# Local attention: the values products one step later on TensorE, the copy of the transposed probabilities after the exponentials on ScalarE

## The chip, the cores and the metric

One core of a Trainium2 chip (trn2). The metric is the device time of one launch in microseconds; the time before is the median of 3 runs. Engines are named as in the profile: PE (TensorE matmul), PEld (its weight loads), DVE (VectorE), ACT (ScalarE), POOL (GpSimd), SP (SyncE, which issues the DMAs here).

## The reference, cut to what matters

`x` is 16 batches of 256 tokens with 128 features. A first phase does one cross-attention over 1601 keys. The second phase, in which everything of this change lies, runs six layers of local attention and a gated FFN:

```python
for i in range(DEPTH):                                   # 6
    x = attn_layer(shift_tokens(x), Wqkv[i], ...) + x
    x = ffn_layer(shift_tokens(x), ...) + x

def attn_layer(x, Wqkv, qs, ksc, Wo):                    # 16 heads of 64
    q, k, v = jnp.split(x @ Wqkv, 3, -1)
    q, k = l2norm(q) * qs, l2norm(k) * ksc               # then rotated by position
    out = local_attention(q, k, v)                       # windows of 32, own and previous
    return out @ Wo

def local_attention(q, k, v):
    sim = jnp.einsum('bhwie,bhwje->bhwij', bq, bk2) * QK_SCALE
    attn = jax.nn.softmax(jnp.where(mask, -big, sim), -1)
    return jnp.einsum('bhwij,bhwje->bhwie', attn, bv2)
```

## The kernel before, in words

The program is written engine by engine. Each engine runs its own list of instructions in order, and semaphores tie the lists together. In the second phase all engines step through the same function `iteration(A, B, C, D)`: four batches are in flight, one in each role. A is projected to q, k and v, squared for its norms and rotated. B has its scores and softmax. C gets the tail of its attention, the output product and the start of its FFN. D gets the end of its FFN. Roles shift by one batch for each iteration: 6 layers of 16 batches make 96 iterations with a B.

An iteration has 8 steps `k`. The attention of a batch is cut into 8 units of four heads by 128 queries; units 0 to 3 (t = 0) are the first half of the tokens, 4 to 7 (t = 1) the second. Unit `u` goes through five stages, and `unit_at(B, C, k, lag)` says which unit stands in step `k` at a stage that lags by `lag` steps (below zero it is one of C):

- `scores` (PE, L1360 and L1369, tiles of 64*64 of the array) writes bank `b_sc`, in step u. The 8 products have 128 columns for t = 0 and 96 for t = 1, as has the mask product ahead of them in each pair (256 and 192).
- DVE takes the maxima (L1268) and makes the biases `nb` (L1277); then ACT does four exponentials with their sums (L1144), in step u. They wait for `nb_ready`, and for `pt_done` of unit u-2, since `probs` has two buffers.
- DVE inverts the sums (L1213) and POOL scales the probabilities (L1068), lag 1.
- `transposes` (PE, L1381, 128*128) turns them into bank `b_pt`, of which there is one; ACT copies it to `probsT` (L1131), which has two buffers. Lag 2.
- `values` (PE, L1401, tiles of 128*64) multiplies `probsT` with `v` into half of the bank `b_o` (the half by u % 2): 8 products of 64 columns for t = 1, 4 of 128 for t = 0; the trace shows each fp32 product as two matmuls. Lag 2. DVE copies `b_o` to `oT` after each second unit (L1205, `keep_o`, lag 3, even steps), and an even unit waits for the copy before it (`o_kept`).

Around these stand, on PE: the projections of A (L1442 in steps 0 to 3, L1453 in 4 to 7), the norms (L1417, steps 2 and 4), the transposed norms (L1464, step 5), the last FFN product of D (L1473, step 0), the output product of C (L1483, steps 1 and 3), two LayerNorm products (L1488, L1492, steps 4 and 5) and the first FFN product (L1513, steps 6 and 7). On ACT: the squares (L1158), logarithm and exponential of the norms (L1109, L1116), copies of v (L1166), and once per iteration the Gelu (L1183) between two loads of a function table (L1183, L79), of which the second stands ahead of the exponentials of step 0. On DVE: the rotations (L1247, L1253), the copy `oT` and the vector parts of the FFN, as `xg` (L1302).

Of the kernel before, what the change touches and what calls it, by code (L numbers as in the profile page):

```python
# [14 lines left out]
ACT = mybir.ActivationFunctionType  # L15
# [753 lines left out]
def ffn_phase(nc, xn_scr, x1_scr, rk_scr, ident, identb, ins, out, NB, DEPTH):  # L769
    with ExitStack() as ctx:  # L770
# [37 lines left out]
        probsT = sb("probsT", [P, 2, 512])  # L808
# [51 lines left out]
        def count(name, n, c, back=0):  # L860

            return n * per[name] + (AHEAD - back) * per[name] + c
# [6 lines left out]
        def unit_at(B, C, k, lag):  # L869

            return (B, k - lag) if k >= lag else (C, UNITS + k - lag)
# [222 lines left out]
        @block.scalar  # L1094
        def _(act):
            s = sems
            start_ahead(act, "act")
            act.wait_ge(setup, N_SETUP)
            act.wait_ge(consts_in, 16 * N_CONSTS)
            nc.scalar.activation(gate_t[:, :], gate[:, :], ACT.Tanh).then_inc(gate_ready, 1)  # L1100
            load_tables(nc, act, EXP_LN_TABLES)

            def iteration(A, B, C, D, begin=None):
                def inverse_norms(i, dst):
                    n = A[0]
                    act.wait_ge(s["norm_done"], count("norm_done", n, i + 1))

                    act.wait_ge(s["rn_ready"], count("rn_ready", n, i))
                    nc.scalar.activation(ln_n2[:, :], b_nv[:, :], ACT.Ln, bias=eps_c[:, 1:2],  # L1109
                                         scale=LN_SCALE).then_inc(s["ln_ready"], 1)  # L1110
                    act.wait_ge(s["ln_ready"], count("ln_ready", n, i + 1))
                    if i == 0:
                        act.wait_ge(s["rk_out"], count("rk_out", n, 0))
                    else:
                        act.wait_ge(s["rqt_done"], count("rqt_done", n, 0))
                    nc.scalar.activation(dst[:, :], ln_n2[:, :], ACT.Exp, bias=eps_c[:, 2:3],  # L1116
                                         scale=-0.5).then_inc(s["rn_ready"], 1)

                for k in range(STEPS):
                    if C and k == 5:  # L1120
                        n = C[0]
                        act.wait_ge(s["xc_done"], count("xc_done", n, 1))
                        act.wait_ge(s["var_done"], count("var_done", n, 1, back=1))
                        nc.scalar.activation(xsq[:, :], b_c[:, S:2 * S], ACT.Square).then_inc(s["xsq_ready"], 1)
                    row, u = unit_at(B, C, k, 2)
                    if row:
                        n = row[0]
                        act.wait_ge(s["pt_done"], count("pt_done", n, u + 1))

                        act.wait_ge(s["o_done"], count("o_done", n, u - 1))  # L1130
                        nc.scalar.activation(probsT[:, u % 2, :], b_pt[:, :], ACT.Copy).then_inc(s["pt_kept"], 1)  # L1131
                    if D and k == 0:

                        load_tables(nc, act, EXP_LN_TABLES)
                    if B:
                        n, _, p, _ = B
                        t, j0 = k // 4, 2 * (k % 4)
                        c0, w = C0[t], P - C0[t]
                        act.wait_ge(s["nb_ready"], count("nb_ready", n, k + 1))

                        act.wait_ge(s["pt_done"], count("pt_done", n, k - 1))
                        for e in range(2):
                            for h in range(2):
                                last = nc.scalar.activation(  # L1144
                                    probs[:, t, k % 2, 2 * e + h, c0:P], b_sc[:, 512 * e + h * w:512 * e + (h + 1) * w],
                                    ACT.Exp, bias=nb[:, k % 2, e, h:h + 1], scale=rq[:, p, t, j0 + h, e:e + 1],
                                    accum_out=psums[:, k % 2, 2 * e + h:2 * e + h + 1])
                        last.then_inc(s["exp_ready"], 1)
                    if A and k == 2:
                        inverse_norms(0, rn_k)  # L1150
                    if A and k < 4:
                        n = A[0]
                        for i in (2 * k, 2 * k + 1):

                            act.wait_ge(s["rotc_ready"], count("rotc_ready", n, i + 1))

                            act.wait_ge(s["norm_done"], count("norm_done", n, i // 4))
                            nc.scalar.activation(sq[:, i % 4, :], b_qk[:, 512 * (i % 2):512 * (i % 2 + 1)], ACT.Square  # L1158
                                                 ).then_inc(s["sq_ready"], 1)
                    if A and 4 <= k < 7:  # L1160
                        n, _, p, _ = A
                        i, e = k - 4, k % 2

                        act.wait_ge(s["o_done"], count("o_done", n, UNITS, back=2))
                        act.wait_ge(s["v_done"], count("v_done", n, i + 1))
                        nc.scalar.activation(v[:, p, i // 2, e * 512:(e + 1) * 512], b_qk[:, e * 512:(e + 1) * 512],  # L1166
                                             ACT.Copy).then_inc(s["v_kept"], 1)
                    if A and k == 4:
                        inverse_norms(1, rn_q)
                    if C and k == 5:  # L1170
                        n = C[0]
                        act.wait_ge(s["var_done"], count("var_done", n, 1))
                        act.wait_ge(s["rstd_ready"], count("rstd_ready", n, 1, back=1))
                        nc.scalar.activation(ln_v[:, :], b_c[:, 0:S], ACT.Ln, bias=eps_c[:, 0:1]
                                             ).then_inc(s["lnv_ready"], 1)
                        act.wait_ge(s["lnv_ready"], count("lnv_ready", n, 1))
                        act.wait_ge(s["xg_ready"], count("xg_ready", n, 1, back=1))
                        nc.scalar.activation(rstd[:, :], ln_v[:, :], ACT.Exp, scale=-0.5).then_inc(s["rstd_ready"], 1)
                if C:
                    n = C[0]  # L1180
                    act.wait_ge(s["h_kept"], count("h_kept", n, 3))
                    act.wait_ge(s["hh_ready"], count("hh_ready", n, 1, back=1))
                    nc.scalar.activation(gg[:, :], gt[:, :], ACT.Gelu).then_inc(s["gelu_ready"], 1)  # L1183
            rows(act, lambda layer: None, iteration)
# [156 lines left out]
        def _(pe):  # L1341
            s = sems
# [4 lines left out]
            def iteration(A, B, C, D, begin=None):  # L1347
# [36 lines left out]
                def values(row, u):  # L1384
                    n, _, p, _ = row
                    t, j0 = u // 4, 2 * (u % 4)
                    pe.wait_ge(s["v_kept"], count("v_kept", n, 3))
                    pe.wait_ge(s["v3_kept"], count("v3_kept", n, 1))
                    if t == 1:
                        pe.wait_ge(s["vmid_in"], count("vmid_in", n, 32))  # L1390

                    pe.wait_ge(s["o_kept"], count("o_kept", n, u // 2))
                    pe.wait_ge(s["pt_kept"], count("pt_kept", n, u + 1))
                    for h in range(2):
                        o0 = (u % 2) * 2 * P + h * P
                        for tile, q0, q1 in V_USE[t]:
                            for e in range(2):
                                r = slice(e * DH, (e + 1) * DH)
                                vc = slice((2 * (j0 + h) + e) * DH, (2 * (j0 + h) + e + 1) * DH)
                                c = (2 * e + h) * P  # L1400
                                last = nc.tensor.matmul(b_o[r, o0 + q0:o0 + q1], v[:, p, tile, vc],  # L1401
                                                        probsT[:, u % 2, c + q0:c + q1], start=True, stop=True,
                                                        skip_group_check=True)
                    last.then_inc(s["o_done"], 1)
# [16 lines left out]
                for k in range(STEPS):  # L1421
                    if B:
                        scores(k)
                    row, u = unit_at(B, C, k, 2)
                    if row:
                        transposes(row, u)
# [33 lines left out]
                    if A and k == 5:  # L1460
# [2 lines left out]
                        for i in range(4):  # L1463
                            last = nc.tensor.transpose(b_nv[:, i * P:(i + 1) * P], rn_q[:, i * P:(i + 1) * P], ident[:, :])  # L1464
                        last.then_inc(s["rqt_done"], 1)
                    if row:
                        values(row, u)
                    if D and k == 0:
                        n, loaded = D[0], D[3]
                        pe.wait_ge(part_in[PART_2], loaded)  # L1470
# [199 lines left out]
```

## Time and profile before

| | us |
|---|---|
| median of 3 runs | 5797.53 (5788.45 to 5801.63) |
| the profiled execution | 5784.99 |
| its span | 5783.2 |
| stretch of the second phase, 2100 to 5700 of the span | 3600.00 |
| PE busy in it | 3478.76 |
| ACT busy in it | 2883.59 |
| DVE busy in it | 2226.03 |
| POOL busy in it | 2194.72 |

The first phase ends at about 2040. From there on PE is the fullest engine. Its granted clock was 1.00 in the stretch. "Busy" counts matmuls from start to a modelled end, so neighbouring groups overlap a little: the time that a group takes is read from its start to the start of the next. A row of the timeline gives the start, the time from the first start to the last end, engine and line, the shapes, and in brackets how long the engine sat idle before and what ended that.

### The profile page before, as it was taken

Reading aid. Unit: us, or ns where it says so; the run is one execution under the profiler, and the core shown is the slowest. Engines: PE = TensorE matmul, PEld = TensorE weight load, DVE = VectorE, ACT = ScalarE, POOL = GpSimd, SP = SyncE. Lnnn points to the kernel's source line nnn. Section 1 sums busy time; section 2 is a strip of 40 time slices with the busy share of each in tenths; the row PEclk is TensorE's granted clock in tenths of the full one; section 3 lists DMA queues with packets and bytes.
Section 4 is the critical chain, followed back from the end, with each engine's and each line's share of the span. In section 5 each row is a group of like instructions: output and inputs, shape, how many; then the busy total and the mean of one; then the engine's idle time right before and its main releaser. Section 6 shows DMA issues by size and latency. Waiting matters only on the chain.

```text
span 5783.2 us, 146589 instructions
## 1 busy us (share of the span) xinstructions
PE 5490.1 (95%) x51848; PEld 3278.6 (57%) x51848; DVE 3631.9 (63%) x8009; ACT 3995.5 (69%) x10790; POOL 2653.2 (46%) x2284
## 2 busy tenths in 40 slices
PE   5999999999999789999999999999999999999997
PEld 2444444444444356666666666666666666666665
DVE  3666776677667456666666666666666666656664
ACT  2555555555555478787887778787888788878885
POOL 2211221112211166656665666666666666665663
PEclk9999999999999899999999999999999999999999
DMA  3232222222332133333333333333333333333332
GB/s 85 61 71 74 57 73 67 74 64 66 74 75 63 54 103 97 100 104 108 97 100 99 108 100 101 94 109 103 102 93 108 104 104 93 97 115 103 93 98 89
DMA packets 144825, 517.35 MB, mean 89 GB/s; under 512 B 29884, under 2 KB 46140, under 8 KB 125676
## 3 DMA queue, kind: packets, MB, share of 16 engines
q1 hardware_dynamic: 142572, 507.58, 31.0%
q8 instruction: 427, 7.00, 0.5%
q14 instruction: 290, 2.38, 0.1%
q10 hardware_dynamic: 1536, 0.40, 0.0%
HBM read 224.98 MB, written 30.68 MB: 44 GB/s over the span
## 4 chain that ended last, share of the span: by engine, by line
PE 44%; ACT 12%; issue 6%; DVE 2%; POOL 1%; DMA 0%; SPq 0%; ACTq 0%; DVEq 0%; POOLq 0%
PE b_qk L1442 9%; PE b_c L1483 6%; PE b_pt L1381 5%; PE b_o L1401 5%; ACT probs L1144 5%; PE b_sc L1369 4%; PE b_nv L1417 3%; PE b_qk L1453 3%; PE b_sc L1360 2%; ACT L1183 2%; ACT L79 2%; PE b_c L1513 2%; PE b_nv L1513 1%; ACT ln_n L1109 1%; PE b_c L1488 1%
## 5 line engine op out<-in xcount | busy, mean ns | idle before, releaser
L436 ACT ACTIVATE eT<-b_e 128x512 f32<-128x512 f32 (+1 forms) x1664 | 903.2, 594 | 871.5 <-PE b_e L754 751.2
L1144 ACT ACTIVATE probs<-b_sc,nb,rq 128x96 f32<-128x96 f32 (+1 forms) x3072 | 1322.5, 449 | 8.7 <-DVE nb L1277 7.5
L509 DVE CUSTOM_DVE_ANT_0 junk<-b_s,mq 128x1024 bf16<-128x1024 f32 (+1 forms) x1024 | 998.9, 990 | 373.3 <-PE b_s L736 359.1
L1068 POOL TENSOR_TENSOR probs<-probs,rsums 128x512 f32<-128x512 f32 (+1 forms) x768 | 717.2, 934 | 666.4 <-DVE rsums L1213 665.9
L1268 DVE TENSOR_REDUCE b_sc<-b_sc 128x4 f32<-128x512 f32 (+1 forms) x768 | 486.1, 633 | 837.6 <-PE b_sc L1369 837.5
L1131 ACT ACTIVATE probsT<-b_pt 128x512 f32<-128x512 f32 x768 | 455.9, 594 | 579.7 <-PE b_pt L1381 579.7
L1442 PE MATMUL b_qk<-xs,weights 128*128 128x256 f32 x3072 | 740.3, 384 | 59.5 <-ACT sq L1158 31.8
L750 PE MATMUL b_e<-mk,identb 128*128 128x512 bf16 (+1 forms) x1664 | 636.7, 383 | 20.6 <-ACT eT L436 19.9
L1144 ACT ACTIVATION_READ_ACCUMULATOR probs<-b_sc,nb,rq 128x1 f32 x3072 | 645.9, 210 | 0.0
L754 PE MATMUL b_e<-q_op,k_op 75*128 75x256 bf16 (+1 forms) x3328 | 639.8, 273 | 0.0
L1442 PEld LDWEIGHTS b_qk<-xs,weights 128*128 128x128 f32 x3072 | 556.4, 191 | 144.9 <-issue 74.5
L1401 PEld LDWEIGHTS b_o<-probsT,v 128*64 128x64 f32 x9216 | 373.0, 137 | 453.3 <-issue 453.3
L1247 DVE TENSOR_TENSOR rot_s<-b_qk,rot_tab 128x512 f32<-128x512 f32 x768 | 525.3, 684 | 127.2 <-PE b_qk L1442 114.7
L1037 POOL TENSOR_TENSOR kT<-kT,rot_p 128x1024 f32<-128x1024 f32 x192 | 454.6, 2368 | 306.1 <-DMA rot_p<-rot_s 302.5
L1401 PE MATMUL b_o<-probsT,v 128*64 128x64 f32 (+1 forms) x9216 | 515.7, 247 | 34.2 <-DVE oT L1205 26.9
L736 PE MATMUL b_s<-k_op,q_op 72*128 72x512 bf16 (+1 forms) x2048 | 504.0, 343 | 27.2 <-DVE smax L509 13.7
L1158 ACT ACTIVATE sq<-b_qk 128x512 f32<-128x512 f32 x768 | 439.1, 599 | 125.1 <-DVE kT L1253 65.5
L656 PE MATMUL b_pv<-eT,vx 128*9 128x256 f32 x6656 | 518.1, 383 | 2.8 <-ACT eT L436 2.8
L1381 PE MATMUL b_pt<-ident,probs 128*128 128x128 f32 x3072 | 504.0, 287 | 1.1 <-POOL probs L1068 1.1
L1045 POOL TENSOR_TENSOR kT<-kT,rkb 128x1024 f32<-128x1024 f32 x192 | 452.1, 2355 | 110.8 <-DMA rkb<-rk_scr 110.8
L1037 POOL TENSOR_TENSOR qT<-qT,rot_p 128x1024 f32<-128x1024 f32 x192 | 453.0, 2359 | 89.5 <-DMA rot_p<-rot_s 70.4
L754 PEld LDWEIGHTS b_e<-q_op,k_op 75*128 75x128 bf16 (+1 forms) x3328 | 332.4, 100 | 252.5 <-issue 5.2
(133 smaller groups left out, 8348.8 us busy)
## 6 DMA issues: line engine op xcount, KB each, us to landing
rot_p<-rot_s SPq DMA_DIRECT2D x768, 256.0 KB, 2.4
rkb<-rk_scr SPq DMA_DIRECT2D x192, 512.0 KB, 6.4
k_op<-k_scr SPq DMA_DIRECT2D x192, 300.2 KB
v<-v SPq DMA_DIRECT2D x192, 256.0 KB, 3.6
k_scr<-kp SPq DMA_DIRECT2D x48, 400.2 KB, 3.5
weights<-in_ffn_w SPq DMA_DIRECT2D x27, 512.0 KB, 5.0
ctxT<-in_ctx SPq DMA_DIRECT2D x17, 800.5 KB, 8.7
q_op<-q_scr SPq DMA_DIRECT2D x144, 64.0 KB
```

Source lines behind the costliest of these rows:

```text
L436: nc.scalar.activation(eT[0:n, g % 2, i * 512:(i + 1) * 512], b_e[i][0:n, :], ACT.Exp).then_inc(s["e_ready"], 1)
L509: nc.vector.tensor_tensor_reduce(junk[:, half, 0:n], b_s[u % 2][:, 0:n], mq[:, p, qt, half * 1024:half * 1024 + n], 1.0, LOWEST, ALU.add, ...
L656: last = nc.tensor.matmul(b_pv[32 * h:32 * h + DK + 1, 0:S], vx[0:n, p, kt, 4 * q + h, :], eT[0:n, g % 2, h * S:(h + 1) * S], start=(kt == ...
L750: nc.tensor.matmul(b_e[i][0:n, :], identb[0:n, 0:n], mk[0:n, p, kt, :].unsqueeze(1).to_broadcast([n, 2, S]), start=True, stop=False, skip_ ...
L754: last = nc.tensor.matmul(b_e[i][0:n, j * S:(j + 1) * S], k_op[q][0:MROW + 3, 2 * i + j, kt * P:kt * P + n], q_op[0:MROW + 3, p, 4 * q + 2 ...
L1037: nc.gpsimd.tensor_tensor(dst, dst, rot_p[:, i % 2, :].rearrange("p (j t) -> p j t", j=4), ALU.add).then_inc(s["sum_ready"], 1)
L1068: nc.gpsimd.tensor_tensor(pu, pu, rsums[:, u % 2, :].unsqueeze(2).to_broadcast([P, 4, w]), ALU.mult).then_inc(s["pn_ready"], 1)
L1144: last = nc.scalar.activation(probs[:, t, k % 2, 2 * e + h, c0:P], b_sc[:, 512 * e + h * w:512 * e + (h + 1) * w], ACT.Exp, bias=nb[:, k % ...
L1247: nc.vector.tensor_tensor(per_block(rot_s[:, q % 2, 512 * (i % 2):512 * (i % 2 + 1)]), per_block(src), rot_tab[:, tab + 1, :].unsqueeze(1) ...
L1381: last = nc.tensor.transpose(b_pt[:, i * P:(i + 1) * P], probs[:, t, u % 2, i, :], ident[:, :])
L1401: last = nc.tensor.matmul(b_o[r, o0 + q0:o0 + q1], v[:, p, tile, vc], probsT[:, u % 2, c + q0:c + q1], start=True, stop=True, skip_group_c ...
L1442: last = nc.tensor.matmul(b_qk[:, 512 * (i % 2) + x * S:512 * (i % 2) + (x + 1) * S], weights[:, c0:c0 + P], xs[:, p, :], start=True, stop ...
```

## The change

Two pieces of code move, and nothing is added or taken away. On PE `values` now has lag 3, and stands right behind `scores` of the step instead of behind the projections. On ACT the copy to `probsT` stands behind the exponentials of its step instead of before them.

```diff
@@ scalar engine, step k
-                    row, u = unit_at(B, C, k, 2)
-                    if row:
-                        n = row[0]
-                        act.wait_ge(s["pt_done"], count("pt_done", n, u + 1))
-
-                        act.wait_ge(s["o_done"], count("o_done", n, u - 1))
-                        nc.scalar.activation(probsT[:, u % 2, :], b_pt[:, :], ACT.Copy).then_inc(s["pt_kept"], 1)
                     if D and k == 0:
 
                         load_tables(nc, act, EXP_LN_TABLES)
...
                         last.then_inc(s["exp_ready"], 1)
+                    row, u = unit_at(B, C, k, 2)
+                    if row:
+                        n = row[0]
+                        act.wait_ge(s["pt_done"], count("pt_done", n, u + 1))
+
+                        act.wait_ge(s["o_done"], count("o_done", n, u - 1))
+                        nc.scalar.activation(probsT[:, u % 2, :], b_pt[:, :], ACT.Copy).then_inc(s["pt_kept"], 1)
                     if A and k == 2:
                         inverse_norms(0, rn_k)
@@ tensor engine, step k
                     if B:
                         scores(k)
+                    row, u = unit_at(B, C, k, 3)
+                    if row:
+                        values(row, u)
                     row, u = unit_at(B, C, k, 2)
                     if row:
                         transposes(row, u)
...
-                    if row:
-                        values(row, u)
                     if D and k == 0:
```

On PE, steps 7 and 0 of one iteration and the next stood before as follows (`b_sc` scores, `b_pt` transposes, `b_qk` projections of A, `b_o` values, then FFN products of C and D):

```order
8711 L1360 MATMUL b_sc<-lmask,identb 64x192 x4
8712 L1369 MATMUL b_sc<-kT,qT 64x96 x8
8713 L1381 MATMUL b_pt<-ident,probs 128x128 x4
8714 L1453 MATMUL b_qk<-weights,xs 128x512
8715 L1401 MATMUL b_o<-probsT,v 64x64 x8
8716 L1513 MATMUL b_c<-xg,weights 128x256 x2
8717 L1360 MATMUL b_sc<-lmask,identb 64x256 x4
8718 L1369 MATMUL b_sc<-kT,qT 64x128 x8
8719 L1381 MATMUL b_pt<-ident,probs 128x128 x4
8720 L1442 MATMUL b_qk<-xs,weights 128x256 x4
8721 L1401 MATMUL b_o<-probsT,v 64x64 x8
8722 L1473 MATMUL b_nv<-hT,weights 128x256 x3
```

The same two steps in the changed kernel, whose lines are shifted by up to three:

```order
8761 L1360 MATMUL b_sc<-lmask,identb 64x192 x4
8762 L1369 MATMUL b_sc<-kT,qT 64x96 x8
8763 L1401 MATMUL b_o<-probsT,v 64x64 x8
8764 L1381 MATMUL b_pt<-ident,probs 128x128 x4
8765 L1456 MATMUL b_qk<-weights,xs 128x512
8766 L1514 MATMUL b_c<-xg,weights 128x256 x2
8767 L1360 MATMUL b_sc<-lmask,identb 64x256 x4
8768 L1369 MATMUL b_sc<-kT,qT 64x128 x8
8769 L1401 MATMUL b_o<-probsT,v 64x64 x8
8770 L1381 MATMUL b_pt<-ident,probs 128x128 x4
8771 L1445 MATMUL b_qk<-xs,weights 128x256 x4
8772 L1474 MATMUL b_nv<-hT,weights 128x256 x3
```

In every step the values products stand ahead of the transposes now, and are those of the unit before; the projections are followed directly by the 128*128 products that the values stood in front of.

On ACT the same place, from the exponentials of step 7 (96 columns) to those of step 0 (128 columns), stood before as follows (`probsT` the copy, `gg` the Gelu):

```order
1541 L1131 ACTIVATE probsT<-b_pt 128x512
1542 L1144 ACTIVATE probs,psums<-b_sc,nb,rq 128x96 x4
1543 L1183 ACT_TABLE_LOAD
1544 L1183 ACTIVATE gg<-gt 128x768
1545 L1131 ACTIVATE probsT<-b_pt 128x512
1546 L79 ACT_TABLE_LOAD
1547 L1144 ACTIVATE probs,psums<-b_sc,nb,rq 128x128 x4
1548 L1158 ACTIVATE sq<-b_qk 128x512 x2
```

In the changed kernel:

```order
1541 L1137 ACTIVATE probs,psums<-b_sc,nb,rq 128x96 x4
1542 L1148 ACTIVATE probsT<-b_pt 128x512
1543 L1183 ACT_TABLE_LOAD
1544 L1183 ACTIVATE gg<-gt 128x768
1545 L79 ACT_TABLE_LOAD
1546 L1137 ACTIVATE probs,psums<-b_sc,nb,rq 128x128 x4
1547 L1148 ACTIVATE probsT<-b_pt 128x512
1548 L1158 ACTIVATE sq<-b_qk 128x512 x2
```

Between the first exponentials of step 7 and the first of step 0 there is still one copy; it moved from behind the Gelu to ahead of the first table load, and the copy ahead of step 7's exponentials has gone behind them.

## Rows read from the trace of the kernel before

**Rows 1.** The head of the page: span and instructions.
```profile
span 5783.2 us, 146589 instructions
```

**Rows 2.** Waits of PE, 2100 to 5700: us in total, times, longest.
```profile
PE b_sc L1360 <- ACT probs L1144: 57.8, 89, 0.7
PE b_qk L1442 <- ACT sq L1158: 27.3, 93, 0.3
PE b_o L1401 <- DVE oT L1205: 22.9, 93, 0.3
```

**Rows 3.** Timeline of PE, step 7 of an iteration to step 1 of the next.
```profile
4004.13 0.28 PE L1360 MATMUL b_sc<-lmask,identb 64*64 64x192 bf16 x4
...
4004.67 0.66 PE L1381 MATMUL b_pt<-ident,probs 128*128 128x128 f32 x4
4005.16 1.02 PE L1453 MATMUL b_qk<-weights,xs 128*128 128x512 f32 x2
4006.11 0.69 PE L1401 MATMUL b_o<-probsT,v 128*64 128x64 f32 x16
4006.73 1.13 PE L1513 MATMUL b_c<-xg,weights 128*128 128x256 f32 x4
4007.87 0.30 PE L1360 MATMUL b_sc<-lmask,identb 64*64 64x256 bf16 x4
...
4011.50 1.53 PE L1473 MATMUL b_nv<-hT,weights 128*128 128x256 f32 x6
4013.69 0.30 PE L1360 MATMUL b_sc<-lmask,identb 64*64 64x256 bf16 x4 [0.65 <-ACT probs L1144]
```

**Rows 4.** Timeline of ACT, the same steps 7 and 0.
```profile
4005.36 0.60 ACT L1131 ACTIVATE probsT<-b_pt 128x512 f32<-128x512 f32 x1 [2.10 <-PE b_pt L1381]
4005.85 0.43 ACT L1144 ACTIVATE probs<-b_sc,nb,rq 128x96 f32<-128x96 f32 x1
...
4008.93 0.84 ACT L1183 ACTIVATE gg<-gt 128x768 f32<-128x768 f32 x1
4009.68 0.58 ACT L1131 ACTIVATE probsT<-b_pt 128x512 f32<-128x512 f32 x1
...
4011.57 0.46 ACT L1144 ACTIVATE probs<-b_sc,nb,rq 128x128 f32<-128x128 f32 x1
```

**Rows 5.** Timeline of PE, the steps 2 to 7 that follow.
```profile
4022.20 1.07 PE L1417 MATMUL b_nv<-sq,pair_ones 128*32 128x512 f32 x8
...
4025.40 1.97 PE L1442 MATMUL b_qk<-xs,weights 128*128 128x256 f32 x8 [0.29 <-ACT sq L1158]
...
4034.02 0.28 PE L1360 MATMUL b_sc<-lmask,identb 64*64 64x192 bf16 x4
...
4035.05 1.02 PE L1453 MATMUL b_qk<-weights,xs 128*128 128x512 f32 x2
4035.91 0.60 PE L1464 MATMUL b_nv<-ident,rn_q 128*128 128x128 f32 x4
...
4037.77 0.28 PE L1360 MATMUL b_sc<-lmask,identb 64*64 64x192 bf16 x4
...
4040.07 0.69 PE L1401 MATMUL b_o<-probsT,v 128*64 128x64 f32 x16 [0.25 <-DVE oT L1205]
4040.69 1.13 PE L1513 MATMUL b_c<-xg,weights 128*128 128x256 f32 x4
4041.66 1.03 PE L1513 MATMUL b_nv<-xg,weights 128*128 128x256 f32 x4
```

**Rows 6.** Timeline of ACT, norms and first square of steps 2 and 3.
```profile
4023.33 0.69 ACT L1109 ACTIVATE ln_n<-b_nv,eps_c 128x512 f32<-128x512 f32 x1 [0.40 <-PE b_nv L1417]
...
4024.68 1.06 ACT L1158 ACTIVATE sq<-b_qk 128x512 f32<-128x512 f32 x2
```

**Rows 7.** Timeline of DVE, step 6.
```profile
4039.12 0.69 DVE L1205 COPY oT<-b_o 128x512 f32<-128x512 f32 x1
4039.73 0.47 DVE L1302 SCALAR_TENSOR_TENSOR xg<-b_c,par,rstd 128x256 f32<-128x256 f32 x1
```

## The prediction

> **What bounds the kernel now.** I read the page first: the span is 5783.2 [rows 1], and the change touches only the part behind 2040. There PE leads with 3478.76 busy of 3600, so I asked for the waits of PE in that stretch. Three rows hold nearly all of them [rows 2]: scores that wait for exponentials (57.8 us), projections that wait for squares (27.3) and values that wait for the copy `oT` (22.9). Each comes some 93 times, once in an iteration, so the timeline of one iteration stands for all.
>
> Step 7 takes 3.74 from scores to scores (4004.13 to 4007.87), step 0 takes 5.82 [rows 3]. The reader is to see that PE works without a gap through step 0 until 4013.03 (4011.50 + 1.53) and then sits idle for 0.65 until ACT is through with the exponentials of step 0. ACT is late there because of a chain without slack from step 7 on: exponentials from 4005.85, load, Gelu at 4008.93, copy at 4009.68, load, exponentials at 4011.57 [rows 4]. The scores of step 0 too start as soon as ACT lets them: exponentials start 4005.85, scores 4007.87, which is 2.02 for four exponentials and the signal. Step 5 (4034.02 to 4037.77, 3.75) is the third of that kind. So of 8 steps, three (7, 0, 5) have the length of the loop scores, DVE and transposes, ACT, scores; the others have the length of PE's own work plus, in steps 3 and 6, one wait.
>
> **The change part by part.** No instruction is added, so the sum consists of starts that shift.
>
> *Steps 7 and 0.* Before, the exponentials started behind the copy: transposes at scores + 0.54, their end 0.66 later, copy, exponentials at scores + 1.72 [rows 3, 4]. Now the copy is out of the way, but the transposes stand behind the values, and the exponentials wait for these transposes (`pt_done`). A values group takes 0.62 from start to next start (4006.11 to 4006.73) [rows 3]. So: 0.54 + 0.62 + 0.66 + 0.03 for the signal (transposes end 4005.33, copy starts 4005.36) = 1.85 after the scores. What was 1.72 becomes 1.85: **+0.13**. The copy that stood in front took 0.49 (4005.36 to 4005.85), the values take 0.62; it is these two that are exchanged. From there to the exponentials of step 0 ACT has the same work as before, one copy, two loads and the Gelu, only in another order: 5.72 (4005.85 to 4011.57) stays [rows 4]. So the 0.65 on PE before step 1 is not won: the copy no longer stands behind the Gelu, but it stands ahead of the first load. The two steps together get 0.13 longer.
>
> The Gelu gets later by a copy, some 0.5 + 0.13, with respect to the scores of step 7. DVE's part of the FFN hangs on it and on its own `oT` copy, and the product L1473 on that. It may move from 4011.50 by some 0.2 to 0.3, but PE has 0.65 of idle time behind it, so this costs nothing; with that cover gone it would cost just these 0.2 to 0.3 in each iteration.
>
> *Step 5.* The same exchange: 0.54 + 0.62 + 0.66 + 0.03 + 2.02 = 3.87 instead of 3.75: **+0.12** [rows 3 to 5].
>
> *Step 6.* Values of an even unit wait here for `oT`, 0.25 by the row, and start at scores + 2.30 (4037.77 to 4040.07) [rows 5]. The new unit in step 6 is odd and stands in the half of `b_o` that was freed long ago: this wait goes. What is late next is `xg`, for which L1513 waits: DVE ends it at 4040.20 (4039.73 + 0.47) [rows 7]. From DVE's end to PE's start the row of `oT` shows 0.26 (4039.12 + 0.69 = 4039.81 to 4040.07) [rows 5, 7]. So L1513 could start at 4040.46 at the latest, by PE's own work at 4040.28 (37.77 + 0.54 + 0.62 + 0.49 transposes + 0.86 projection), against 4040.69 before: between -0.23 and -0.41. I take **-0.30**, a little off the late end. `oT` itself now waits for values of its own step; these end at scores + 1.2 and DVE comes to `oT` at + 1.35 (4037.77 to 4039.12), so it isn't delayed, by 0.1.
>
> *Steps 1 and 3.* These have PE's own length. Their sequence was scores (64*64), transposes and projections (128*128), values (128*64), output product (128*128); now it is scores, values, transposes, projections, output product: one change of tile shape fewer. What such a change costs is in the rows. The projection L1453 to the next group takes 0.95 where values follow (4005.16 to 4006.11), and 0.86 where 128*128 follows (4035.05 to 4035.91) [rows 3, 5]: 0.09 for leaving. And the first four matmuls of L1513 behind values take 1.13, the next four 1.03 [rows 5]: 0.10 for entering. Together **-0.20** in each of these steps, -0.40 for both. The same is won in step 6 (it is in its number) and in 7, 0 and 5, where the loop through ACT hides it. In steps 2 and 4 the norms (128*32) stand between, and the number of changes stays. Bounds: nothing (if the change into 128*64 behind 64*64 costs more than others) and twice as much.
>
> The Trainium skill says this too: on the page "TensorEngine Tiling (Array Packing)", section "Key Properties", a change of tiling mode drains the engine, a change of tile within a mode doesn't. Without a cost for it the sum below would be smaller by 0.40 an iteration; the rows above agree with the page, with 0.09 and 0.10.
>
> The wait of step 3 stays. The projections at 4025.40 wait for squares, these for the norms: norms start 4022.20, logarithm 4023.33, squares 4024.68, projection 4025.40 [rows 5, 6]. Norms are later by 0.62 in their step, and the projection would be too, as values now stand before each; the 3.20 between them are ACT's. ACT was idle 0.40 before the logarithm [rows 6], and the copy falls into that.
>
> *Step 2* gets a unit of the second half with 16 small matmuls instead of 8 larger ones, +0.03; *step 4* nothing. In all steps below 4 the projections, and with them the rotations on DVE, the swap DMAs and POOL's sums, come 0.62 later. Nothing waits closely for them: the squares of step 1 end well before the norms of step 2, POOL's products are due some 3 us later.
>
> **The sum.** +0.13 + 0.12 - 0.30 - 0.40 + 0.03 = -0.42 us an iteration. Over 93 full iterations [rows 2] -39 us. The profiled execution (5784.99, 1.8 above its span [rows 1]) would come to 5746; it is 12.5 below the median of the runs, and from the median 5797.5 I get **5758**.
>
> **The rivals.**
>
> 1. *Shape changes are free in effect* (what is left of -0.42 without the -0.40 is nothing): 5796. For it: the gain rests on 0.1 us effects seen in other neighbourhoods. Against: each is seen in every iteration.
> 2. *Values behind scores cost no drain, and the exponentials follow sooner.* If values can start while the last scores run, 0.1 less in all steps, those of the ACT loop too: -0.8 more an iteration, 5797.5 - 93 * 1.2 = 5685. Against: the transposes behind the same scores start 0.54 after them, at their modelled end less 0.07.
> 3. *Slower: the waits of the values become visible.* `values` has up to five semaphores to pass (both kinds of v, its swapped part, `o_kept`, `pt_kept`). Before, PE's sequencer passed them while the long projections ran; now they stand behind the scores, the shortest group (0.54). A wait that PE meets with an empty queue costs 0.26 (the `oT` row). Half of it exposed in 7 steps is +0.91, net +0.49 an iteration, 5843; all of it +130 us, 5927. It decides from 0.06 a step (0.42 / 7). Against it: the transposes, with two, start behind the same scores without delay. The Trainium skill bears on it in one sentence, "Perfetto Trace Analysis", section "Identifying Dependency Chains": waits beyond one may become instructions of their own ahead of the waiting one; the page gives no price, so by it alone the sum stays.
> 4. *Slower: the later projections find somebody.* The 0.62 later rotations, swaps or sums reach a wait that has no slack. Each 0.45 an iteration cancels the gain: about 5800 to 5830.
>
> **How the numbers follow.** The forecast has 0.52, own range 5725 to 5780 (the bounds of step 6 and of the shape changes). Rival 1 has 0.14, rival 2 0.10, rival 3 0.14, rival 4 0.10. 5700 to 5815 holds the forecast, rival 1, and the near parts of the others; outside are most of rival 2 and the upper half of rival 3. A measurement of this kernel tells 0.2%, some 12 us, from no change. Faster by more than that: forecast, rival 2 and a weak form of rival 4, 0.68. Within it: rival 1 and a bit of 4, 0.14. Slower: 0.18.
>
> **What would show it.** In the profile of the changed kernel: the exponentials of step 7 start 1.85 after the scores, with the transposes as releaser; the idle time before the scores of step 1 is still 0.6 or more; the wait of values for `oT` is gone, and steps 1 and 3 are 0.2 shorter; the row of projections that wait for squares is still there with about 0.3. The prediction is wrong if values start later than 0.54 to 0.67 after the scores of their step, or if a new row of some tens of us stands among PE's waits.

## The result, and the profile after

| | median us | lowest to highest | ratio to before, 95% interval |
|---|---|---|---|
| before | 5797.53 | 5788.45 to 5801.63 | |
| changed | 5764.45 | 5753.66 to 5765.58 | 0.9944 (0.9930 to 0.9959) |
| changed again, beside before at 5791.13 | 5755.02 | 5754.21 to 5766.77 | 0.9942 (0.9928 to 0.9955) |

The change makes the kernel faster by 0.6%, 33 us in the first comparison and 36 in the second. The forecast was 39 us less, 5758.

The waits of PE in the changed kernel, 2100 to 5700, answer to [rows 2] (total us, times, longest):

```profile
PE b_sc L1360 <- ACT probs L1137: 113.2, 276, 2.4
PE b_qk L1445 <- ACT sq L1158: 27.3, 93, 0.3
PE b_nv L1474 <- DVE hT L1229: 19.5, 80, 1.9
PE b_qk L1445 <- POOL xs L1060: 4.4, 5, 1.2
PE b_c L1489 <- POOL xs L1077: 2.4, 11, 0.3
```

The wait for `oT` is gone, the wait for squares is the same to a tenth, and the wait for exponentials has doubled, from 57.8 to 113.2 us, and comes three times in an iteration instead of once. The row of `hT` is new, with 19.5 us. In the same 3600 us PE is busy for 3425.55 instead of 3478.76, so it sits idle 53 us more, and yet the kernel is 33 us faster; whoever reads waits alone gets the sign wrong. PE's own work got shorter. The timeline of PE over steps 7 and 0 shows both:

```profile
4030.87 0.28 PE L1360 MATMUL b_sc<-lmask,identb 64*64 64x192 bf16 x4
4030.98 0.50 PE L1369 MATMUL b_sc<-kT,qT 64*64 64x96 f32 x16
4031.41 0.69 PE L1401 MATMUL b_o<-probsT,v 128*64 128x64 f32 x16
4032.02 0.65 PE L1381 MATMUL b_pt<-ident,probs 128*128 128x128 f32 x4
4032.51 1.02 PE L1456 MATMUL b_qk<-weights,xs 128*128 128x512 f32 x2
4033.37 1.03 PE L1514 MATMUL b_c<-xg,weights 128*128 128x256 f32 x4
4034.79 0.30 PE L1360 MATMUL b_sc<-lmask,identb 64*64 64x256 bf16 x4 [0.39 <-ACT probs L1137]
...
4036.57 1.89 PE L1445 MATMUL b_qk<-xs,weights 128*128 128x256 f32 x8
4038.68 1.53 PE L1474 MATMUL b_nv<-hT,weights 128*128 128x256 f32 x6 [0.22 <-DVE hT L1229]
4040.62 0.30 PE L1360 MATMUL b_sc<-lmask,identb 64*64 64x256 bf16 x4 [0.40 <-ACT probs L1137]
```

Values start 0.54 after the scores and keep the transposes 0.61 off. The projection L1456 gives way to L1514 after 0.86 (0.95 before, where values followed), and L1514 takes 1.03 (1.13 before, behind values) [rows 3]. Then PE sits idle for 0.39. ACT in the same steps:

```profile
4032.78 0.43 ACT L1137 ACTIVATE probs<-b_sc,nb,rq 128x96 f32<-128x96 f32 x1 [1.77 <-PE b_pt L1381]
...
4034.43 0.60 ACT L1148 ACTIVATE probsT<-b_pt 128x512 f32<-128x512 f32 x1
4035.04 1.28 ACT L1183 ACT_TABLE_LOAD   x1
4036.34 0.84 ACT L1183 ACTIVATE gg<-gt 128x768 f32<-128x768 f32 x1
4037.20 1.28 ACT L79 ACT_TABLE_LOAD   x1
4038.50 0.46 ACT L1137 ACTIVATE probs<-b_sc,nb,rq 128x128 f32<-128x128 f32 x1
```

The releaser of the exponentials is `b_pt`, the transposes. They start 1.91 after the scores (4030.87 to 4032.78), and from there to the exponentials of step 0 pass 5.72, to the hundredth what it was [rows 4].

Since the iterations repeat, the length of each step, from the first L1360 of a step to that of the next, can be taken as a median over all 96. The table gives it for both kernels and for the experiments that follow:

| step | 0 | 1 | 2 | 3 | 4 | 5 | 6 | 7 | sum |
|---|---|---|---|---|---|---|---|---|---|
| before | 5.82 | 5.52 | 4.57 | 6.03 | 4.21 | 3.75 | 4.84 | 3.74 | 38.48 |
| changed | 5.83 | 5.33 | 4.60 | 5.83 | 4.22 | 3.91 | 4.48 | 3.92 | 38.11 |
| e1, PE part | 6.01 | 5.33 | 4.60 | 5.83 | 4.32 | 4.32 | 4.48 | 4.35 | 39.24 |
| e2, ACT part | 6.35 | 6.78 | 4.84 | 6.76 | 5.09 | 5.09 | 6.41 | 5.59 | 46.92 |
| e3, values late in 1 and 3 | 5.82 | 5.53 | 4.60 | 6.61 | 4.22 | 3.92 | 4.48 | 3.92 | 39.09 |
| e9, values late in 1 | 5.82 | 5.52 | 4.60 | 5.83 | 4.22 | 3.90 | 4.48 | 3.92 | 38.29 |
| e10, values late in 6 | 5.82 | 5.33 | 4.60 | 5.83 | 4.21 | 3.90 | 5.81 | 3.92 | 39.43 |
| e4, two more waits | 5.82 | 5.33 | 4.60 | 5.83 | 4.21 | 3.92 | 4.52 | 4.02 | 38.25 |
| e5, values at the end of 7 | 5.30 | 5.33 | 4.60 | 5.83 | 4.21 | 3.91 | 4.48 | 4.02 | 37.68 |
| e6, and at the end of 5 | 5.30 | 5.33 | 4.60 | 5.83 | 4.21 | 3.91 | 4.48 | 4.02 | 37.67 |
| e7, and copies of v later | 5.30 | 5.33 | 4.60 | 5.83 | 4.21 | 3.49 | 4.48 | 4.02 | 37.26 |
| e8, no table loads | 5.10 | 5.33 | 4.60 | 5.83 | 4.22 | 3.91 | 4.48 | 3.92 | 37.38 |

### The profile page after: what moved, and what is told of

It is laid out like the page before. It is cut to its first block, busy times and chain, and to the rows that moved or that the text cites. A ratio compares the mean times of both kernels' runs of the same rounds, so it can differ in the third digit from the quotient of the medians.

```text
span 5763.5 us, 146589 instructions
## 1 busy us (share of the span) xinstructions
PE 5421.1 (94%) x51848; PEld 3298.3 (57%) x51848; DVE 3658.0 (63%) x8009; ACT 4000.6 (69%) x10790; POOL 2656.3 (46%) x2284
## 4 chain that ended last, share of the span: by engine, by line
PE 35%; ACT 19%; issue 7%; POOL 2%; DMA 1%; DVE 1%; SPq 0%; ACTq 0%; DVEq 0%; POOLq 0%
ACT probs L1137 9%; PE b_qk L1445 9%; PE b_c L1484 5%; PE b_o L1401 5%; PE b_pt L1381 5%; PE b_sc L1369 3%; ACT L1183 2%; PE b_sc L1360 2%; ACT L79 2%; ACT ln_n L1109 2%; PE b_c L1514 2%; PE b_nv L1417 2%; PE b_nv L1514 1%; PE b_qk L1456 1%; DMA rot_p<-rot_s 1%
## 5 line engine op out<-in xcount | busy, mean ns | idle before, releaser
L1137 ACT ACTIVATION_READ_ACCUMULATOR probs<-b_sc,nb,rq 128x1 f32 x3072 | 618.1, 201 | 0.0
```

The source lines that it names most:

```text
L1137: last = nc.scalar.activation(probs[:, t, k % 2, 2 * e + h, c0:P], b_sc[:, 512 * e + h * w:512 * e + (h + 1) * w], ACT.Exp, bias=nb[:, k % ...
```

## The experiments

The medians of before beside each batch: 5785.60 for e1 to e4, 5789.53 for e5 to e8, 5791.13 for e9 to e11.

### e1: the PE part alone

```diff
-                    (exponentials, then the copy to probsT)
+                    row, u = unit_at(B, C, k, 2)
+                    if row:
+                        ...
+                        nc.scalar.activation(probsT[:, u % 2, :], b_pt[:, :], ACT.Copy)...
+                    (then the exponentials, as before)
```

> The PE part alone: values one step later and behind the scores, the copy to probsT still ahead of the exponentials. Theory (scores, values, transposes, then ACT is a loop that sets steps 7, 0 and 5): the exponentials now stand behind values, transposes and the copy, 0.49 later than in the changed kernel, so step 7 becomes 4.4 (from 3.9), step 5 4.4 (from 3.9), step 4 4.36 (from 4.22), and step 0 keeps its length; 1.1 us an iteration more than the changed kernel, about 5865, slower than before. Rival (the copy's place does not matter, the gain is all PE's own order): 5764, as the changed kernel.

Measured: 5869.11, ratio 1.0139 (1.0122 to 1.0156). Steps 7 and 5 come out at 4.35 and 4.32, step 4 at 4.32, the iteration 1.13 longer than in the changed kernel; 1.1 was expected. PE waits for exponentials 225.2 us:

```profile
PE b_sc L1360 <- ACT probs L1144: 225.2, 272, 1.0
PE b_qk L1445 <- ACT sq L1158: 26.7, 91, 0.3
```

Steps 1, 2, 3 and 6 are the same as in the changed kernel. So these four owe their lengths to PE's part alone, and the copy's new place is worth what it takes out of the loop through ACT. Step 0 was expected to keep its length and got 0.18 longer than in the changed kernel: the copy stands behind the Gelu again, and starts 0.93 after it (4053.94 to 4054.87) instead of 0.75 [rows 4], just behind the end of step 0's transposes at 4054.83, which now stand behind the values.

### e2: the ACT part alone

```diff
                         last.then_inc(s["exp_ready"], 1)
+                    (the copy to probsT here; values stay at lag 2, behind the projections)
```

> The ACT part alone: the copy behind the exponentials, the values still two steps behind the scores and behind the projections. Theory: values must now wait for exponentials and copy of their own step, which end some 3.75 after the scores where they were due at 2.0 to 3.0; every step gets 0.3 to 1.7 longer, 9 us an iteration in sum, about 6650. Rival (the old lag is enough, since the copy moves by less than the projections last): within 1% of before.

Measured: 6677.80, ratio 1.154 (1.1517 to 1.1563). Every step is longer, and the wait is where it was looked for:

```profile
PE b_o L1401 <- ACT probsT L1148: 692.6, 598, 1.8
```

Neither part alone is a gain: one costs 1.4%, the other 15%. The extra step of lag is what lets the copy go behind the exponentials.

### e3 and e9: values behind the projections again, in steps 1 and 3, and in step 1 alone

```diff
                     row, u = unit_at(B, C, k, 3)
-                    if row:
+                    if row and k not in (1, 3):          # e9: (1,)
                         values(row, u)
...
+                    row, u = unit_at(B, C, k, 3)
+                    if row and k in (1, 3):              # behind the projections; e9: (1,)
+                        values(row, u)
```

> The changed kernel, but in steps 1 and 3 the values (the same unit, lag 3) stand behind the projections again. Nothing waits in these steps for values or for the exponentials, so only the number of changes of tile shape differs. Theory (a change of shape costs 0.1 to leave and 0.1 to enter): steps 1 and 3 get 0.20 longer each, 0.40 an iteration, 5764 + 37 = 5801, and the whole gain of the change is gone. Rival (shape changes cost nothing, steps 1 and 3 got shorter for another reason): 5764.

Measured: 5839.47, ratio 1.0091 (1.0074 to 1.0107). By the steps the loss against the changed kernel is 0.98 * 93 = 91 us, where 37 were expected. Step 1 got 0.20 longer, as the theory has it; step 3 got 0.78 longer. The waits say why:

```profile
PE b_qk L1445 <- ACT sq L1158: 80.1, 91, 0.9
```

It was 27.3. The projections of step 3 wait for squares that come a fixed time after the norms of step 2. With the values behind the projections, nothing but scores and transposes stands between norms and projections, and 0.58 of the values' 0.6 turns into waiting. I had missed that in writing the expectation. So step 3 measures two things, and e9 takes step 1 by itself.

> The changed kernel with the values behind the projections in step 1 alone, where e3 had steps 1 and 3. Theory (one more change of tile shape costs 0.20 in step 1, and the rest of what e3 lost came from step 3, where the values no longer stand between the norms and the projections that wait for squares): step 1 5.53, all other steps as in the changed kernel, 0.20 * 93 = 19 us more than it, about 5783. Rival (e3 lost its time otherwise): another step changes, or more than 30 us.

Measured: 5775.89, ratio 0.9973 (0.9964 to 0.9982); the changed kernel beside it has 5755.02 and 0.9942 (0.9928 to 0.9955). Only step 1 changed, 5.33 to 5.52. That is 0.19 * 93 = 18 us by the steps, and 21 by the medians. The trace says where in step 1 it lies. First e9, then the changed kernel:

```profile
4009.28 1.89 PE L1445 MATMUL b_qk<-xs,weights 128*128 128x256 f32 x8
4011.10 0.69 PE L1401 MATMUL b_o<-probsT,v 128*64 128x64 f32 x16
4011.72 1.99 PE L1487 MATMUL b_c<-oT,weights 128*128 128x256 f32 x8
```

```profile
4004.28 1.89 PE L1445 MATMUL b_qk<-xs,weights 128*128 128x256 f32 x8
4006.01 1.89 PE L1484 MATMUL b_c<-oT,weights 128*128 128x256 f32 x8
```

The projections give way to the values after 1.82, and to the output product after 1.73: 0.09 for leaving. The output product takes 1.99 behind the values and 1.89 behind the projections: 0.10 for entering. The values themselves take the same in both places, 0.62 and 0.61. So one visit to another tile shape more in a step costs 0.19 to 0.20 us. Whether the shape itself is the cause, or anything that keeps the next weights from being loaded ahead, these runs do not separate: projections that start behind the wait for squares take 1.97 instead of 1.89 without any change of shape.

### e10: values behind the projections in step 6 alone

The edit is that of e9 with `(6,)`.

> The changed kernel with the values behind the projections in step 6 alone. Theory (in even steps DVE's copy oT waits for the values of its own step, and in step 6 xg and the first FFN product stand behind it, so the place ahead of the transposes is what keeps that free): oT starts 0.7 after the end of the values, about 2.7 after the scores instead of 1.35, and L1513's product 1.3 to 1.5 later: step 6 5.8 to 5.9 instead of 4.48, 125 to 135 us more than the changed kernel, 5895. Rival (only the wait of the values for oT was worth something, and it is gone by the new lag wherever they stand): step 6 0.2 longer, 5783.

Measured: 5887.49, ratio 1.0171 (1.0155 to 1.0186), step 6 5.81. PE in that step:

```profile
4051.06 0.28 PE L1360 MATMUL b_sc<-lmask,identb 64*64 64x192 bf16 x4 [0.40 <-ACT probs L1137]
...
4053.05 0.66 PE L1401 MATMUL b_o<-probsT,v 128*64 128x128 f32 x8
4054.98 1.10 PE L1517 MATMUL b_c<-xg,weights 128*128 128x256 f32 x4 [1.28 <-DVE xg L1302]
```

Values end at 4053.71, and only then DVE can copy `oT` and come to `xg`; the FFN product waits 1.28 for it. The lag of one more step by itself would have lost in step 6, because DVE's copy in an even step is due for the unit of that same step. The place ahead of the transposes keeps this free.

### e4: two more waits ahead of the values

```diff
                 def values(row, u):
...
+                    for x in range(2):
+                        wait_apart(pe, pe_passed, s["v_kept"], count("v_kept", n, 3))
                     pe.wait_ge(s["o_kept"], count("o_kept", n, u // 2))
```

> The changed kernel with two more waits ahead of each values group, both on a semaphore passed long ago, each with an increment of its own. Theory (PE's sequencer passes the waits of the values while the scores run, with room for one or two more): 5764 to 5800, steps 6, 0 and 1 longest hit since their scores start late. Rival (waits behind the short scores are exposed and already cost the changed kernel something): 0.1 to 0.25 more in each step, 5840 to 5950.

Measured: 5768.63, ratio 0.9972 (0.9961 to 0.9982) against before at 5785.60. That is 17 us faster than before, where the changed kernel was 33 and 36 faster in its own comparisons; these runs and those of e11 were made on different chips, so the medians are not set side by side. Two steps are longer, 7 by 0.10 and 6 by 0.04, which is 0.14 * 93 = 13 us. Seven semaphores are nearly free. That the first five are quite free shows in the changed kernel itself: in every step the values start 0.54 after scores of 96 columns and 0.67 after those of 128 (medians), as the transposes with their two did before. Rival 3 of the prediction is refuted: it asked for 0.13 a step from the first five.

### e5, e6, e7: out of the loop through ACT

In e5 the values of step 7 stand at the end of the step, ahead of the next scores. This keeps the number of shape changes and puts the transposes right behind the scores.

```diff
-                    if row:
+                    if row and k not in (7,):            # e6, e7: (5, 7)
                         values(row, u)
...
+                    row, u = unit_at(B, C, k, 3)
+                    if row and k in (7,):                # the last of the step
+                        values(row, u)
```

> The changed kernel, but in step 7 the values stand at the end of the step, behind the first FFN product and right ahead of the next scores: the same number of shape changes, and the transposes stand right behind the scores. Theory (step 7 and 0 have the length of the loop through ACT, and it starts when the transposes behind the values end): the exponentials of step 7 start with the biases, 1.5 after the scores instead of 1.91, and everything up to the scores of step 1 is 0.4 earlier: 38 us less, about 5726, faster than both kernels. Rival (steps 7 and 0 are bound by something else): 5764.

Measured: 5718.55, ratio 0.9879 (0.9864 to 0.9894). On ACT the releaser is DVE's `nb` now, and the run behind is unchanged:

```profile
4002.98 0.43 ACT L1137 ACTIVATE probs<-b_sc,nb,rq 128x96 f32<-128x96 f32 x1 [1.34 <-DVE nb L1277]
...
4008.70 0.46 ACT L1137 ACTIVATE probs<-b_sc,nb,rq 128x128 f32<-128x128 f32 x1
```

4002.98 to 4008.70 is 5.72 again. Steps 7 and 0 together fell from 9.75 to 9.32, by 0.43. Step 7 alone is a little longer, as the FFN product now comes so early that it waits for `gt`:

```profile
PE b_sc L1360 <- ACT probs L1137: 42.0, 94, 2.4
PE b_c L1514 <- DVE gt L1219: 29.3, 90, 0.7
```

> As the one before, with the values of step 5 at the end of their step as well. Theory A (step 5 is bound by ACT's work of step 4: exponentials, copy, copy of v, logarithm and exponential of the norms, square, without a gap up to the exponentials of step 5): no further gain, 5726. Theory B (step 5 is bound as step 7 is, by the transposes behind the values): another 0.4 less, 5688.

Measured: 5713.87, ratio 0.9864 (0.9849 to 0.9879): step 5 stays at 3.91. Theory A holds. In step 5 two bounds lie on top of each other, the transposes behind the values and ACT's unbroken work since step 4, and taking the first away shows nothing.

e7 adds this on ACT:

```diff
-                    if A and 4 <= k < 7:
-                        (copy of v, i = k - 4)
+                    if A and k == 6:
+                        keep_v(2)
...
                         nc.scalar.activation(rstd[:, :], ln_v[:, :], ACT.Exp, scale=-0.5)...
+                    if A and k == 5:
+                        keep_v(0)
+                        keep_v(1)
```

> As the one before, and on ACT the copies of v of steps 4 and 5 stand behind the LayerNorm's work of step 5, so that 0.48 of ACT's work leaves the run from the exponentials of step 4 to those of step 5. Theory A (that run bounds step 5 once the values are out of the way): step 5 falls from 3.9 to about 3.5, 38 us less than the one before, 5688. Theory B (the values were what bound step 5): no difference to the one before.

Measured: 5683.33, ratio 0.9813 (0.9800 to 0.9827). Step 5 falls to 3.49. ACT between the exponentials of steps 4 and 5:

```profile
4016.70 0.60 ACT L1148 ACTIVATE probsT<-b_pt 128x512 f32<-128x512 f32 x1
4017.18 0.70 ACT L1109 ACTIVATE ln_n<-b_nv,eps_c 128x512 f32<-128x512 f32 x1
4017.91 0.72 ACT L1116 ACTIVATE rn_q<-ln_n,eps_c 128x512 f32<-128x512 f32 x1
4018.54 0.36 ACT L1124 ACTIVATE xsq<-b_c 128x256 f32<-128x256 f32 x1
4018.87 0.43 ACT L1137 ACTIVATE probs<-b_sc,nb,rq 128x96 f32<-128x96 f32 x1
```

This version is 1.9% faster than before and beats both kernels.

### e8: without the two table loads

The load L79 is left out, and `ACT.Gelu` is `ACT.Square`, so that no load stands ahead of it either. This kernel computes another FFN and serves for its time alone.

> The changed kernel with Gelu replaced by a square, so that both table loads in an iteration go; it computes another FFN. Theory (the idle time of PE before the scores of step 1 is the ACT run of copy, two loads and Gelu): exponentials of step 0 start with their biases, step 0 has the length of PE's work, 5.0 to 5.1 instead of 5.83, 5764 - 75 = 5690. Rival (the idle time has another cause, DVE or the FFN product): 5764.

Measured: 5694.73, ratio 0.9833 (0.9818 to 0.9849). Step 0 is 5.10, where 5.0 to 5.1 was expected, and no other step moved. So the idle time before the scores of step 1, 0.40 of the 0.73 that step 0 lost here, is ACT's run with the two loads. Most of the rest is the wait for `hT`, 0.22 in the changed kernel, which hangs on the Gelu and is gone too.

### e11: the changed kernel again

> The changed kernel again, beside the two before on one chip. Both theories: within 0.2% of its first median, 5764.

Measured: 5755.02, 0.16% off its first median; the table at the head has its ratio.

## Why the prediction was right

The size came out as 33 and 36 us, where 39 was forecast, and the steps of the table let each term be read by itself.

- **Steps 7 and 0**, forecast +0.13: measured 9.56 to 9.75, +0.19. The mechanism is the one named: e1 lengthens the loop by the copy, e5 takes the values out of it and gets 0.43 back. The size was off by the signal from the transposes to the exponentials. I had put 0.03, the distance to the copy in [rows 3, 4]; in the changed kernel the transposes end at 4032.67 and the exponentials start at 4032.78, 0.11. Hence 1.91 after the scores instead of the 1.85 that were to be seen.
- **"The 0.65 is not won"**: right. Step 0 is 5.83 after 5.82. PE's idle time before step 1 is 0.40 instead of 0.65 only because PE comes later to it: L1474 now waits 0.22 for `hT`, which is late by the copy that stands ahead of the Gelu. The cover that the prediction named holds; the row of 19.5 us costs nothing. Two of the signs in the prediction contradict this part of it: with L1474 later by 0.26 the idle time had to fall to 0.4, where the list says 0.6 or more, and `hT` had to become a row of some twenty us, where the list takes a new row as a sign of being wrong.
- **Step 5**, forecast +0.12: +0.16. The size is near, the bound was named wrongly, and that is luck. The prediction took step 5 for a loop through the transposes, as step 7. Before, the copy in step 5 had no idle time ahead of it (2.10 in step 7) and stood right behind `xsq`; ACT had worked without a gap since the exponentials of step 4 at 4031.53:

```profile
4034.56 0.66 PE L1381 MATMUL b_pt<-ident,probs 128*128 128x128 f32 x4
```

```profile
4035.01 0.36 ACT L1124 ACTIVATE xsq<-b_c 128x256 f32<-128x256 f32 x1
4035.28 0.59 ACT L1131 ACTIVATE probsT<-b_pt 128x512 f32<-128x512 f32 x1
4035.76 0.43 ACT L1144 ACTIVATE probs<-b_sc,nb,rq 128x96 f32<-128x96 f32 x1
```

  In the changed kernel the same work stands between the same exponentials, 4.25 instead of 4.23, and starts later because the exponentials of step 4 wait for transposes behind values:

```profile
4020.14 0.43 ACT L1137 ACTIVATE probs<-b_sc,nb,rq 128x96 f32<-128x96 f32 x1 [1.25 <-PE b_pt L1381]
...
4024.39 0.42 ACT L1137 ACTIVATE probs<-b_sc,nb,rq 128x96 f32<-128x96 f32 x1
```

  Step 4's exponentials moved from 1.72 to 1.88 after their scores (4018.26 to 4020.14), and step 5's with them, from 1.74 to 1.91 (4022.48 to 4024.39). The transposes of step 5 end at 4024.26 and would have allowed nearly the same start, 4024.37 with the 0.11 of above. e6 and e7 told the two apart; ACT's rows of the kernel before already could.
- **Step 6**, forecast -0.30: -0.36. The late bound, `xg`, held, with a shorter signal: `xg` ends at 4028.83 (4028.35 + 0.48) and L1514 starts at 4028.97, 0.14 later, where the sum took 0.26 from the row of `oT`. `oT` was not late for the values of its own step, as argued; e10 shows what it would have cost.
- **Steps 1 and 3**, forecast -0.20 each: -0.19 and -0.20. e9 shows it for step 1, with the 0.09 and 0.10 in the places that were named. For step 3 the claim that the wait for squares stays was right (27.3 us before and after), but the reason goes further than I wrote: in e3 the values' time there is needed to cover it.
- **Steps 2 and 4**, +0.03 and 0: +0.03 and +0.01.

The sum by steps is -0.37 instead of -0.42, times 93 is 34 us. Single iterations and the end of the program go the other way, and the sum had no term for them. In 15 of the changed kernel's iterations (16 in its second profile, 4 before) step 4 is 0.1 to 0.3 longer, when POOL's copy `xs` comes late for L1489 (84.5 us in the row of its weight loads, 18.8 before):

```profile
PEld b_c L1489 <- POOL xs L1077: 84.5, 94, 1.2
```

That is a weak form of rival 4, about 3 us by the steps. It fits that there are 4 again in e3, where the projections of steps 1 and 3 do not stand behind values, but how the delay reaches POOL was not tested. From the start of the last step with scores to the end of the span pass 47.4 us (45.6 in the second profile), 43.3 before. The two profiled executions are only 19.8 us apart (5784.99 and 5765.24), and their mean granted clocks differ too, 0.993 and 0.990; the changed kernel's one run at 0.993 took 5753.66, 31 less. Rival 1 is refuted by e9, rival 2 by the distance of values behind the scores (0.54), rival 3 by e4.

## What to carry to other kernels

When a tiled group (here 128*64) is moved, count the changes of tile shape in the row of groups before and after: grouped so that one change falls away, steps 1 and 3 got 0.2 us shorter each. Steps 1, 3 and 6 gained 0.75 us an iteration, these two 0.39 of it; the other steps took 0.38 back. Whatever is put between a producer and the engine that closes the loop back to it lengthens that loop: place such a group by the step's bound, early where PE or a third engine bounds the step, at the end where the loop does (e5), and expect a second bound right behind the first (e6). A lag added for one consumer moves the due time of all others: DVE's `oT` stayed free with the values ahead of the transposes and did not with the values behind the projections (e10).

## What the hardware showed that I had not expected

The clock of PE fell for some microseconds in the middle of the second phase of the changed kernel, where before it stayed at full clock. Busy time of each engine, the granted clock and DMA in four microseconds of the changed kernel:

```profile
3951.00:3955.00 4.00, 3.67 (x39) 2.60 (x40) 0.84 (x3) 0.00 (x0) 2.70 (x4) 0.50 0.00 0
```

0.50 is 1.2 GHz. The matmuls show it:

```profile
3948.68 1.10 PE L1514 MATMUL b_c<-xg,weights 128*128 128x256 f32 x4 [0.61 <-DVE xg L1302]
3949.62 1.40 PE L1505 MATMUL b_nv<-par,weights 128*128 128x1 f32 x12
3951.34 2.07 PE L1514 MATMUL b_nv<-xg,weights 128*128 128x256 f32 x4 [0.33 <-DVE bias L1308]
```

The last row takes 2.07 instead of the 1.03 of an ordinary iteration. It is the third iteration of a layer, where PE makes the layer's bias from 12 products of one column and waits for DVE; the same place of the kernel before ran at full clock. Ahead of the fall stand the wait of 0.61 for `xg` and those narrow products. The second profile of the changed kernel has the same at 3953 to 3957, with a mean granted clock of 0.58, and once more one layer later, at 4567.

The kept traces say more. The place comes six times in a run. Over the twelve traces without e2 (whose clock falls all through the stretch), there is no wait for `xg` in 43 of these places, and the clock falls in none of them; there is one, of 0.51 to 1.40 us, in 29, and the clock falls in 11. It falls nowhere else between 2100 and 5600. e1 and e3 have the values in their new place as well, never show the wait here, and never the fall. e3 in the same layer, at a granted clock of 1.00:

```profile
3991.96 1.10 PE L1517 MATMUL b_c<-xg,weights 128*128 128x256 f32 x4
3992.90 1.40 PE L1508 MATMUL b_nv<-par,weights 128*128 128x1 f32 x12
3994.62 1.13 PE L1517 MATMUL b_nv<-xg,weights 128*128 128x256 f32 x4 [0.33 <-DVE bias L1308]
```

So the fall goes with the wait for `xg` ahead of the narrow products, and the change brings the wait in three of six layers. Why it falls in 11 of 29 such places and not in the others stays open, and no run was made to test it. In the first profile steps 6 and 7 of that iteration took 3.2 us more than in the layers without the wait, of which 0.6 stand as well in the last layer, with the wait and without the fall.
